# Three products of constants ahead of each wait for the low halves of the probabilities, in the third and fourth layer's attention

## What is computed

```python
x = L0_attn_x                      # (16, 256, 128)
xn = _layernorm(x);  x = x + attention_n(xn) + feed_forward_n(xn)      # n = 0, 1, 2, 3
```

```python
logits = jnp.einsum('bhsd,bhtd->bhst', q, k) * scale
logits = jnp.where(mask, logits, neg_inf)
probs = jax.nn.softmax(logits, axis=-1)
out = jnp.einsum('bhst,bhtd->bhsd', probs, v)
```

```python
scores = jnp.einsum('bqhd,bkhd->bhqk', q, k)
scores = scores + jnp.einsum('bqr,bkr->bqk', q_rope, k_rope)[:, None]
w = jax.nn.softmax(jnp.where(causal, -jnp.inf, scores / scale), axis=-1)
attn = jnp.einsum('bhqk,bkhd->bqhd', w, v)
```

## Time and profile before

| of the profiled execution | |
|---|---|
| time of the execution | 2516.36 us |
| span from the first to the last instruction | 2514.2 us |
| mean granted TensorE clock | 0.844 |
| TensorE products busy | 1907.0 us (76%) |
| VectorE busy | 1575.3 us (63%) |
| ScalarE busy | 1221.9 us (49%) |
| POOL busy | 1139.9 us (45%) |
| A2, first to last start of line 768 | about 1201.7 to 1597.5 us |
| A3, the same | about 1853.6 to 2285.6 us |

### The profile page before, as it was taken

How to read it: one execution, slowest core, us unless ns; L and a number is a source line. 1 busy time by engine, 2 the same in 40 slices (tenths; PEclk the granted TensorE clock), 3 DMA queues, 4 the chain that set the end, 5 groups by cost and what they waited for, 6 DMA issues and landing times.

```text
span 2514.2 us, 61783 instructions
## 1 busy us (share of the span) xinstructions
PE 1907.0 (76%) x21198; PEld 1363.1 (54%) x21199; DVE 1575.3 (63%) x3649; ACT 1221.9 (49%) x2607; POOL 1139.9 (45%) x921
## 2 busy tenths in 40 slices
PE   1553799999999788805888888683768787777998
PEld 0223466666667566604566666462535555555666
DVE  2236788787888788856444444475655555554774
ACT  0232577676777555501555555552235455554553
POOL 0003477675555233320775555342036775543551
PEclk9785799999999899955677776696777878988999
DMA  8900000011000011120111113021043333420223
GB/s 228 178 0 0 11 17 17 18 40 46 2 2 2 26 47 47 57 71 19 51 53 33 32 30 94 17 60 56 1 105 98 99 104 92 104 79 26 62 63 116
DMA packets 165195, 138.38 MB, mean 55 GB/s; under 512 B 17128, under 2 KB 151368, under 8 KB 164976
## 3 DMA queue, kind: packets, MB, share of 16 engines
q1 hardware_dynamic: 151312, 107.24, 17.2%
q0 software_dynamic: 11584, 23.91, 2.8%
q10 hardware_dynamic: 2080, 4.19, 0.5%
HBM read 57.84 MB, written 52.01 MB: 44 GB/s over the span
## 4 chain that ended last, share of the span: by engine, by line
PE 47%; DVE 20%; issue 11%; POOL 11%; ACT 8%; DMA 2%; DVEq 1%; SPq 1%; ACTq 0%; POOLq 0%
PE duo L1167 12%; PE mo L1167 9%; POOL v L768 7%; PE ob L1167 7%; PE misc L1167 7%; PE acc L1167 6%; PE pt L1167 3%; ACT v L1040 3%; DVE nmax L2288 2%; ACT v L1039 2%; DVE v L1973 2%; DVE region L2291 1%; DVE v L1965 1%; POOL rstd L736 1%; DVE stats L1795 1%
## 5 line engine op out<-in xcount | busy, mean ns | idle before, releaser
L768 POOL TENSOR_TENSOR v<-v 128x768 f16<-128x768 f32 x256 | 419.7, 1640 | 461.6 <-ACT v L1040 459.6
L763 POOL TENSOR_TENSOR v<-v 128x512 f16<-128x512 f32 x256 | 290.5, 1153 | 257.1 <-DVE region L2291 256.8
L790 POOL DMA_INDIRECT results<-probT,dest_no x202 | 217.2, 1075 | 329.8 <-ACT probT L822 289.3
L1167 PE MATMUL ob<-wm,v 128*128 128x9 f16 (+1 forms) x5856 | 257.4, 180 | 107.5 <-POOL v L768 86.3
L1167 PEld LDWEIGHTS ob<-wm,v 128*128 128x128 f16 x5856 | 215.3, 99 | 190.6 <-POOL v L768 93.7
L2180 DVE TENSOR_REDUCE nm<-duo 128x2 f16<-128x256 f32 x256 | 108.8, 425 | 294.8 <-PE duo L1167 294.7
L1039 ACT ACTIVATE v<-mo 128x384 f32<-128x384 f32 x352 | 174.3, 495 | 205.4 <-PE mo L1167 203.2
L1102 ACT ACTIVATE v<-mo 128x512 f32<-128x512 f32 x256 | 153.4, 599 | 157.7 <-PE mo L1167 157.7
L2288 DVE TENSOR_REDUCE nmax<-duo 128x2 f32<-128x512 f32 x256 | 164.9, 686 | 82.5 <-PE duo L1167 82.5
L1167 PE MATMUL duo<-kT,wm 128*128 128x256 f16 x1212 | 172.6, 279 | 56.0 <-DVE kT L1961 30.4
L1040 ACT ACTIVATE v<-mo 128x384 f16<-128x384 f32 x352 | 175.6, 499 | 0.0
(11 more groups left out here) (318 smaller groups left out, 4376.6 us busy)
## 6 DMA issues: line engine op xcount, KB each, us to landing
prob<-slot_rows SPq DMA_DIRECT2D x101, 130.0 KB, 2.2
head_rows<-v SPq DMA_DIRECT2D x96, 128.0 KB
load<-wm SPq DMA_DIRECT2D x32, 384.0 KB
qT<-results SPq DMA_DIRECT2D x40, 256.0 KB, 3.1
qT<-wm SPq DMA_DIRECT2D x16, 384.0 KB
slot_rows<-prob SPq DMA_DIRECT2D x4, 1300.0 KB, 19.4
slot_rows<-prob SPq DMA_DIRECT2D x4, 1235.0 KB, 19.7
kT<-head_rows SPq DMA_DIRECT2D x40, 96.0 KB
```

Source lines behind the costliest of these rows:

```text
L763: pool.tensor_tensor(p16[:, p % 2, h, 1, :], p32[:, h, :], p16[:, p % 2, h, 0, :], ALU.subtract)\
L768: pool.tensor_tensor(p16_2[:, p % 2, 1, :], p32_2[:, p % 2, :], p16_2[:, p % 2, 0, :], ALU.subtract)\
L790: pool.indirect_dma_start(out=results[layer], out_offset=bass.IndirectOffsetOnAxis(ap=dest_no[:, 2 * b + t:2 * b + t + 1], axis=0), in_=y_ ...
L1167: return pe.matmul(dst, lhsT, rhs, start=start, stop=stop)
```

## The change

Ahead of each wait for the low halves, and behind the wait for `o_made` where there is one, TensorE issues three products of the identity and the mask, taken twice side by side: 256 columns in bf16, written to columns 256 to 511 of `ob`. Each starts an accumulation of its own and ends it. Nothing reads these columns. The function is used by A2 and A3; it is called 128 times in each.

```diff
                     g, b, jj = pair2(p)
                     if p % 4 == 0:
                         at_step(o_made, pe, stage, i, g - 1)
+                    for _n in range(3):
+                        mm(ob[:, SEQ:CHUNK].rearrange("p (a c) -> p a c", a=2), ident16[:, :], twice(mask16[:, :]),
+                           True, True)
                     p_low.wait(pe, stage, i, p)
                     for h in range(2):
                         for qt in range(2):
```

## The result

| | before | after |
|---|---|---|
| median of four runs | 2512.78 us | 2441.2 us |
| range of the runs | 2503.85 to 2516.45 | 2436.25 to 2445.64 |
| time of the profiled execution | 2516.36 us | 2445.64 us |
| mean granted TensorE clock | 0.844 | 0.905 |
| A2, first to last start of line 768 | 395.8 us | 354.5 us |

The ratio is 0.972, with a 95% interval of 0.9687 to 0.9752. All of it lies in the two stages: they are 41.3 and 30.4 us shorter, and what lies around them is the same to 1.5 us.

A forecast was written before the change was run, and what follows sets the result against it. Bound: a latency loop in both attention stages, TensorE's clock having a 16% share. A risen clock gives 45 us, preparations cost 9, so 36 less: 2480 for the profiled execution, 2476 as median; 8-in-10 range 2460 to 2504.

The forecast's parts named there:

- the price of the clock in A2: Second layer's attention: full clock saves 4.9 us in the first two chunks and 27.4 us from the third on.
- The 9 us for the preparations: Steps with a chunk's projections mixed in: added products delay them, 7 us in A3 and 2 us in A2.
- The clock: Both attention stages: added wide products raise TensorE's granted clock, A2 from 0.68 and 0.70 to near 1.0, A3 above 0.95.
- The loop: Attention steps: a latency loop closing over two steps, 6.09 us per pair in A2, 5.14 at full clock.
- The POOL floor: A2's first two chunks, A3's first four: POOL's 2.82 us period lets a pair fall only to 5.64 us.
- I take zero: Plain steps at full clock: the added products lengthen neither of the two chains, so they cost nothing.
- Pairs go from 6.09 to 5.14, 15.6%: A2 from its third chunk: 176 us at half clock gain 15.6%, which makes 27.4 us.
- 6 us, at the bottom of the range: Full-precision products of turns and projections, taking twice their time at half clock, give 6 us in the 2460 case.
- 12.8 us by the clock less 7: A3: the clock saves 6.5 us in the first four chunks and 6.3 in the last four; preparations cost 7.
- Rival 1: Clock rises, but A3's stalls drop it repeatedly and half the half-clock time stays: 15.5 us less, 2496; chance 17%.
- Rival 2: Clock follows idle gaps and stays; TensorE bounds each pair at 6.66 us against 6.09: 44 us more, 2556; chance 6%.
- Rival 3: Clock rises, but averages after the short distance carry their delay into both chains, 42 us against 45: 2509; chance 7%.

The follow-up runs named there:

- run 5: The changed kernel with each of the three added products 16 columns wide instead of 256: 2501.31 us, ratio 0.9938 to the kernel before.
- run 7: The changed kernel with the three products using one row of the array instead of 128, still 256 columns: 2628.52 us, ratio 1.0469 to the kernel before.
- run 6: The changed kernel with the three products moved behind the wait for the low halves, ahead of the average: 2473.04 us, ratio 0.9825 to the kernel before.
- runs 3 and 4: VectorE's low halves of the rotated rows set to zero, in the kernel before (2488.39 us) and in the changed kernel (2435.27 us).

## Why the prediction was right in kind and too small

Two steps of it failed. The larger is a term that it put at nothing: what VectorE's meetings with POOL cost A3, 16 to 18 us. The other is the price of the clock in A2, put at 32 us, where the stage is 41.3 shorter. The 9 us for the preparations were too dear as well. All three point the same way. By stages, A2 was forecast to be 30 us shorter, products paid, and is 11 beyond that; A3 was forecast at 6, and is 8.5 beyond that by clock and preparations and 16 by the meetings. With the 36 forecast this makes the 71 us.

**The clock: right.** PEclk near 1.0 in A2 and above 0.95 in A3 was forecast and came. In these kernels the level goes with how much wide, full-height work TensorE streams, not with its busy figure: run 5 (narrow) and run 7 (one row) show it from two sides.

**The loop: right.** Forecast were pairs of 5.14 us; they take 5.07. The POOL floor of 2.82 us in A2's first two chunks holds too: there its starts now follow each other by 2.81 to 2.84 in 24 of 32 steps.

**"I take zero" for the products in plain steps: right.** They stand in the waits or before the average with time to spare, and run 6 shows the price of the other place. The preparing steps had a term of their own, which follows.

**The 9 us for the preparations: too dear.** In A3's fourth to sixth step, where I had a delay of 0.33 in two of three, the steps took 3.65, 3.35 and 3.57 us before and 3.71, 3.35 and 3.64 after: 0.13 us per chunk, 1 us in all.

**The size of the clock's gain in A2: a term mis-sized.** "Pairs go from 6.09 to 5.14, 15.6%" was taken from bare steps and laid over all of the time at half clock. 41.3 us came from 222 us of it, 18.6%. By stretches, A2's first two chunks gave 9.6 us where the sum had 4.9, and the rest 31.7 where it had 27.4. Much of this lies in two of a chunk's steps: summed over the chunks, the sixth went from 35.5 to 26.7 us and the eighth from 35.6 to 27.9, 16.5 us together, where 15.6% of all of their time would be 11.1. The sixth holds the fp32 products of the values, the eighth the fp32 projection of the finished output. The chain of the kernel before through one at half clock, and that of the changed kernel at full:

```profile
1467.49 0.59 PE ob L1167 x18
1468.09 0.95 PE duo L1167 x6
1469.04 1.71 PE acc L1167 x8
```
```profile
1357.86 0.61 PE ob L1167 x18
1358.47 0.57 PE duo L1167 x6
1359.04 0.89 PE acc L1167 x8
```

Eight fp32 products stand in the chain with 1.71 or 0.89 us: such a step gains 0.82 beside the 0.48 of a bare one. I had put all such products at 6 us, at the bottom of the range; with 14 pieces of eight in A2, up to 11.5 us hang on them, if every one stood in the chain at half clock. That the whole of the difference is this is argued from the sizes; no run tested it alone.

**A3: a mechanism missed.** Forecast were 12.8 us by the clock less 7, measured 30.4. The clock's part was near: 14.3 between runs 3 and 4. The other 16 to 18 us are the meetings. This term the prediction put at nothing without a reason. It had the row in hand, TensorE's wait of up to 3.6 us for the turned maxima, and used it only as cover for the products. It never asked why VectorE was late. One look at the durations of a single line of VectorE, 683 ns at the median and 2604 at most, would have shown that much of its time was not work. That the change would turn the meetings in its favour could not have been read from the kernel before: there the same start, 0.39 us ahead of POOL, went the other way. That it gained by them is luck; that they were there to be gained was readable.

**The rivals.** Rival 1 took A3's stalls for a brake on the clock; they were a gain not yet counted. Rival 2 didn't come, but run 7 shows that it was priced too low: 7.36 us per pair at half clock with products of that length, not 6.66. Rival 3 was the price of a place in the chain, and run 6, behind the wait, paid just that: 0.32 us per pair.

## What to carry to other kernels

Where a loop has waits on TensorE and its granted clock stands at 0.5 with a high busy figure, wide full-height products of constants in those waits can lift the clock; put them ahead of the wait, and stop at the number that still fits (three here). Price a clock by the longest TensorE pieces in the chain, not by the plain step alone. And where the longest execution of one line takes four times its median, find what ran beside it on another engine before you take the wait behind it as given. Such a meeting can turn with a small change of pace, so count it separately: the part of a gain that comes from it may not come again in another kernel.

## What the runs showed of the hardware

**Rows at work count for the clock here.** Three products of 256 columns and 128 rows per step gave 0.98 in A2; the same with one row gave 0.64, and three of 16 columns 0.73; with none it was 0.70. Products of an identity and a mask are enough to lift it.

**VectorE and POOL exclude each other in some operations.** A VectorE operation with two SBUF operands that meets POOL's with two either runs its 0.68 us, and then POOL's takes 1.78 to 2.12 us instead of 1.65 (in the changed kernel's seven it ends 1.50 us behind VectorE's end), or it waits and ends 0.55 us behind POOL's end. The changed kernel shows the first case, VectorE and then POOL:

```profile
1894.39 0.70 DVE L2126 TENSOR_TENSOR prob<-prob 128x512 f32<-128x512 f32 x1
1895.59 0.68 DVE L2131 TENSOR_TENSOR wm<-prob,wm 32x512 f16<-32x512 f32 x1
```
```profile
1895.98 1.79 POOL L768 TENSOR_TENSOR v<-v 128x768 f16<-128x768 f32 x1
```

The Trainium skill, page SBUF — State Buffer, section Who interferes with whom, names just this pair of operations as one of those that share an exclusive lock; the trace agrees. It also says that whoever issues first holds it. Here the rows disagree: with VectorE's start 0.39 us ahead, VectorE lost four times of four in the kernel before (1939.48 against 1939.87) and won three of three after (1895.59 against 1895.98). So the recorded start alone does not decide it. One thing goes with the outcome in all 12 kernels here that have the operation. Over A3 they have 45 meetings with VectorE's start 0.39 to 0.41 us ahead. VectorE lost the 12 in which the sum before it (line 2123 before, 2126 after; also two SBUF operands) had itself been held up to 0.93 us or more, and won the 33 in which that sum took 0.89 us or less; the rows above have 1.15 and 0.70. Why that should count stays open, and no run varied it alone.
